# Three cross attentions opened inside the drains of the stages in front of them, in a twelve-stage decoder on one core

## The reference, cut to what matters

```python
x = _layernorm(x + _L0_attn_ref(x, ...))              # differential attention
x = _layernorm(x + _L0_xattn_ref(x, ctx_768, ...))    # scores clipped at 10000
x = _layernorm(x + _L0_ffn_ref(x, ...))               # two of eight experts
x = _layernorm(x + _L1_attn_ref(x, ...))              # rotary attention
x = _layernorm(x + _L1_xattn_ref(x, ctx_768, mask_BxS2_bf1, ...))
x = _layernorm(x + _L1_ffn_ref(x, ...))
x = _layernorm(x + _L2_attn_ref(x, ...))              # causal linear attention
x = _layernorm(x + _L2_xattn_ref(x, ctx_768, ctx_768, ...))
...

def _L2_xattn_ref(query, key, value, ...):
    Qp = query @ Wq + bq
    K = _l2norm(key @ Wk + bk)
    V = value @ Wv + bv
    Q = _l2norm(Qp)
    scores = jnp.einsum('bhqd,bhkd->bhqk', Q, K) * SCALE
    attn = jax.nn.softmax(scores, axis=-1)
    out = jnp.einsum('bhqk,bhkd->bhqd', attn, V)
    out = out @ Wo + bo
    x = out + Qp
    return (x - mu) / jnp.sqrt(var + LN_EPS) * ln_gamma + ln_beta
```

## Time and profile before

| what | value |
|---|---|
| median of 3 runs | 1764.18 us |
| lowest and highest | 1756.68 and 1767.77 us |
| the profiled execution | 1762.84 us, of which the span is 1761.1 us |
| TensorE (PE) busy in the span | 1565.7 us, 89% |
| VectorE (DVE), ScalarE (ACT), GpSimd (POOL) | 908.0, 679.4 and 412.6 us |
| mean granted TensorE clock | 0.959 of full speed |
| chain of waits, share by engine | PE 70%, DVE 11%, issue 8%, DMA 4% |

### The profile page before, as it was taken

How to read it: one execution, slowest core, us unless ns; L and a number is a source line. 1 busy time by engine, 2 the same in 40 slices (tenths; PEclk the granted TensorE clock), 3 DMA queues, 4 the chain that set the end, 5 groups by cost and what they waited for, 6 DMA issues and landing times.

```text
span 1761.1 us, 40069 instructions
## 1 busy us (share of the span) xinstructions
PE 1565.7 (89%) x14932; PEld 1292.9 (73%) x14932; DVE 908.0 (52%) x2316; ACT 679.4 (39%) x1611; POOL 412.6 (23%) x627
## 2 busy tenths in 40 slices
PE   7998998789995879998699598897998999999998
PEld 6876777678994757776589476775786776789897
DVE  3665787521105557777311363457444555565764
ACT  3334776322333327654123222553563443311110
POOL 2223776510005431111100243442121111000101
PEclk9998999999997999999899798999999999999999
DMA  5443000178971011110587201111001010033232
GB/s 204 148 153 135 28 27 16 49 291 293 319 250 46 1 42 41 30 29 12 229 293 275 75 1 33 41 40 49 1 1 62 28 42 1 25 111 105 88 104 69
DMA packets 41852, 166.76 MB, mean 95 GB/s; under 512 B 5984, under 2 KB 16864, under 8 KB 30176
## 3 DMA queue, kind: packets, MB, share of 16 engines
q1 hardware_dynamic: 39392, 159.14, 25.8%
q0 software_dynamic: 2304, 5.51, 1.0%
HBM read 140.22 MB, written 24.41 MB: 93 GB/s over the span
## 4 chain that ended last, share of the span: by engine, by line
PE 70%; DVE 11%; issue 8%; DMA 4%; POOL 3%; ACT 3%; SPq 1%; DVEq 0%; POOLq 0%; ACTq 0%
PE bank L1968 7%; PE bank L1981 7%; PE bank L1382 4%; PE bank L1910 4%; PE bank L1912 4%; PE bank L1911 4%; PE bank L1369 3%; PE bank L866 2%; PE bank L857 2%; PE bank L831 2%; PE bank L958 2%; PE bank L1352 2%; PE bank L1396 1%; PE bank L1357 1%; PE bank L1612 1%
## 5 line engine op out<-in xcount | busy, mean ns | idle before, releaser
L3597 POOL TENSOR_TENSOR mv<-mv,cst 112x1 f32<-112x1 f32 x88 | 22.5, 255 | 584.2 <-DVE mv L2631 584.2
L2336 ACT ACTIVATE arena<-big,nm 112x375 f32<-112x375 f32 x256 | 143.9, 605 | 25.9 <-DVE nm L3282 15.9
L2550 ACT ACTIVATE htile<-bank,wup 128x128 f32<-128x128 f32 x280 | 79.7, 368 | 189.6 <-PE bank L1968 189.6
L1968 PE MATMUL bank<-xtile,wup 128*128 128x128 f32 x1120 | 132.9, 278 | 0.3 <-DVE xtile L3444 0.2
L1382 PEld LDWEIGHTS bank<-cst,arena 112*125 112x125 f32 x768 | 100.1, 196 | 44.5 <-issue 21.9
L1968 PEld LDWEIGHTS bank<-xtile,wup 128*128 128x128 f32 x1120 | 129.9, 194 | 1.0 <-DVE xtile L3444 0.9
L3460 DVE COPY yrow<-bank 128x256 f32<-128x256 f32 x35 | 14.9, 425 | 217.6 <-PE bank L1981 217.6
L1981 PE MATMUL bank<-wdn,htile 128*128 128x256 f32 x560 | 126.3, 379 | 0.0
L1382 PE MATMUL bank<-cst,arena 112*125 112x112 f32 x768 | 115.3, 289 | 8.3 <-POOL arena L3763 4.7
L1981 PEld LDWEIGHTS bank<-wdn,htile 128*128 128x128 f32 x560 | 103.9, 190 | 12.8
L3763 POOL TENSOR_SCALAR arena<-arena,c_lo 112x375 f32<-112x375 f32 x64 | 98.0, 1544 | 37.1 <-ACT c_lo L2340 36.9
(11 more groups left out here) (386 smaller groups left out, 3735.8 us busy)
## 6 DMA issues: line engine op xcount, KB each, us to landing
wup<-in_moe_up SPq DMA_DIRECT2D x35, 1028.0 KB, 7.5
wdn<-in_moe_dn SPq DMA_DIRECT2D x35, 1024.0 KB, 5.5
vspace<-in_ring SPq DMA_DIRECT2D x40, 512.0 KB, 3.9
ctxs<-parts SPq DMA_DIRECT2D x30, 564.0 KB, 3.8
slots<-mlpw SPq DMA_DIRECT2D x11, 1024.0 KB, 6.3
parts<-ctxs SPq DMA_DIRECT2D x8, 564.0 KB, 3.1
xrow<-slots SPq DMA_DIRECT2D x35, 128.0 KB, 5.0
slots<-yrow SPq DMA_DIRECT2D x35, 128.0 KB, 7.1
```

What stands on the lines that cost most here:

```text
L1968: mm = pe.matmul(bank[2 + 2 * (g % 2) + m // 4][:, m % 4 * ROWS:(m % 4 + 1) * ROWS], wup[:, g % 3, k * HID + 128 * m:k * HID + 128 * m + 1 ...
L2336: nc.scalar.activation(c_pr[:, g, j, :], c_sc[:, g % 2, j, :], ACT.Exp, bias=nm[:, p, h:h + 1], scale=-1.0).then_inc(cexp_done, 1)
L2550: ins = nc.scalar.activation(htile[:, g % 2, m, :], bank[2 + 2 * (g % 2) + m // 4][:, m % 4 * ROWS:(m % 4 + 1) * ROWS], func, bias=wup[:, ...
```

## The change

It takes the code that opens stages 1, 4 and 7 out of these stages and puts it, cut into named pieces, into the drains of stages 0, 3 and 6, on TensorE, ScalarE, VectorE and GpSimd. The pieces replace filler matmuls. Some PSUM banks of the drains are changed to make room. The `split_kv` of stages 3 and 6 moves from the end of the stage to the end of step 1. In stage 7 ScalarE does its four exponentials in a run, and TensorE makes the first half of the next keys behind the values instead of in front of them. The core of the diff:

```diff
@@ TensorE, diff, step @@
-                            for _ in range(4):
-                                warm(bank[4], 512)
+                            cross(SUBS[sub.index + 1], "keys")
+                            cross(SUBS[sub.index + 1], "more keys")
                             pe.wait_ge(ln_dve, START + 3 * ln_unit(sub, b - 2) + 1)
                         output_columns_d(b - 1)
+                        if not back[0]:
+                            cross(SUBS[sub.index + 1], "queries")
@@ TensorE, causal, drain @@
                     if one:
-                        output_rows(sub, b - 1, bank[2])
-                        fillers(3)
-                        output_columns(sub, b - 1, bank[2])
+                        output_rows(sub, b - 1, OT)
+                        cross_normed(SUBS[sub.index + 1], "first")
+                        output_columns(sub, b - 1, OT)
+                        cross_normed(SUBS[sub.index + 1], "second")
+                        rows_t(sub, b - 2, p, bank[5])
+                        project_rows(sub, b - 1, OT)
+                        fillers(4)
                     else:
-                        fillers(3)
-                    rows_t(sub, b - 2, p, bank[5])
-                    if one:
-                        fillers(1)
-                        project_rows(sub, b - 1, bank[2])
+                        cross_normed(SUBS[sub.index + 1], "third")
+                        rows_t(sub, b - 2, p, bank[5])
+                        cross_normed(SUBS[sub.index + 1], "fourth")
@@ TensorE, rope, drain @@
                         values_turned(sub, b - 1, 1 - p)
+                        pe.wait_ge(xt_done, xt_at(sub, b - 3))
+                        cross(SUBS[sub.index + 1], "keys")
...
+                        output_rows(sub, b - 1, OT)
+                        cross(SUBS[sub.index + 1], "more keys")
+                        output_columns(sub, b - 1, OT)
+                        cross(SUBS[sub.index + 1], "queries")
+                        project_rows(sub, b - 1, OT)
+                        fillers(2)
@@ TensorE, cross_normed, pieces @@
+                if piece == "first":
+                    wait_weights(pe, sub)
+                    query_rows(0, 0)
+                    pe.wait_ge(part_low, B + 1 + sub.index // 3)
+                    keys(0, 0, 0, bank[0])
+                    return
+                if piece == "second":
+                    keys(0, 0, 1, bank[1])
+                    return
+                if piece == "third":
+                    pe.wait_ge(ln_dve, START + 3 * ln_unit(before, B - 2) + 1)
+                    queries_t(0, 0, TL)
+                    return
+                if piece == "fourth":
+                    key_sums(0, bank[4])
+                    return
@@ TensorE, cross_normed, step t = 0 @@
                             query_rows(b + 1, 1 - p)
-                            pe.wait_ge(cv_done, at(sub, "c3", b, 0))
-                            pe.wait_ge(cq_done, at(sub, "c1", 0, 1))
-                            keys(b + 1, 1 - p, 0, bank[5])
...
+                        if more:
+                            if one:
+                                pe.wait_ge(cv_done, at(sub, "c3", b, 0))
+                            else:
+                                wait_rows(pe, sub, B - 1)
+                            keys(b + 1, 1 - p, 0, bank[5])
@@ ScalarE and VectorE, rope and causal, step @@
-                    if isinstance(b, int) and b == B - 1:
+                    if isinstance(b, int) and b == 1:
                         split_kv(SUBS[sub.index + 1])
@@ VectorE, causal, drain @@
                     if one:
-                        output_normed(sub, b - 1, bank[2])
+                        output_normed(sub, b - 1, OT)
                     else:
-                        split_kv(SUBS[sub.index + 1])
+                        cross_normed(SUBS[sub.index + 1], "third")
                     rows_out(sub, b - 2, p)
@@ ScalarE, cross_normed, step @@
-                        exps(b, t, p, (0, 1))
-                    if t in (0, 1) and more:
+                        exps(b, t, p, (0, 1, 2, 3))
+                    if t == 1 and more:
                         keys(b + 1, 1 - p, t, bank[5])
...
+                    if back[0] and t < 2:
+                        value_rows(b, p, t, (TL, bank[4])[t])
+                    if t == 0 and more:
+                        keys(b + 1, 1 - p, t, bank[5])
@@ GpSimd, diff and rope, step @@
+                    if one and not back[0]:
+                        cross(SUBS[sub.index + 1], "queries")
```

181 lines of the change are left out of this document (115 added, 66 removed).

## The result

| | before | changed |
|---|---|---|
| median of the runs beside each other | 1765.97 us (4 runs, 1756.68 to 1767.99) | 1745.18 us (4 runs, 1735.58 to 1745.63) |
| ratio | | 0.9883, 95% interval 0.9844 to 0.9922 |
| profiled execution, span, clock | 1762.84, 1761.1, 0.959 | 1745.63, 1743.8, 0.956 |

The change makes the kernel 20.8 us faster, 1.2%. The forecast was 1743.0, out of terms that sum to -21. In a second comparison the changed kernel had 1739.8 us (6 runs) against 1763.4 (11 runs), ratio 0.987 (0.9841 to 0.9898).

What follows compares the result with a forecast made beforehand. TensorE was taken to be simply busy for most of the program, except in passages between stages. Terms -3.5, -6.55, +2.8, -8.7 and -5.0 gave -20.95, say -21 us, forecast 1743.0 us, range 1731 to 1755.

Steps and rivals of the forecast that it cites:

- Stage 0 to 1: Passage into stage 1: 4.5 us taken away, queries in front of the last projection cost 1.04; sum -3.5 us.
- Stage 3 to 4: Passage into stage 4: 5.95 us go, the split leaving the drain gives -0.9, longer queries cost +0.3; sum -6.55 us.
- The split in stage 3: Moved to step 1: VectorE waits for ScalarE's cast, delaying row 2's maxima; +2.8 us, bounds 0 and +4.5.
- rival A: Fewer fillers let TensorE's clock fall to half after pauses, taking some gain back: -11 us or 1753; chance 0.27.
- Stage 6 to 7: Passage into stage 7: 8.4 us removed, last rows_t 0.7 later, full clock -1.0; together -8.7 us, bounds -5.5 and -11.
- two-input rule: Stage 6's drain: normed queries on VectorE and GpSimd's root might exclude each other over SBUF; queries priced 0.35 to 1.6 us.
- Stage 7's loop: Context waits -6.1 and exponential waits 1.3 go, second keys' copy 1.2 later; -5.0 us, bounds -7.4 and +2.
- Elsewhere: Stages outside the edited ones: no term in the sum, since later weights and contexts are asked for by events that move along.
- signs of being wrong: Starts move but not the end, half clock in more stretches, or TensorE waits on stage 7's copy of keys.
- B: Stage 3's split finds VectorE free and half clock after the passage into stage 1 stays away: -26.3 us or 1737; chance 0.15.
- C: Stage 7's loop: later key copies chain up to 6.2 us per row over seven rows: +27 us or 1791; chance 0.05.
- D: Gains are waited for again at a load or in routing behind stages 1 and 4: about -8 us or 1756; chance 0.05.

Runs made afterwards that it cites:

- run 7: Changed kernel with the next stage's queries behind the last projection in stage 3's drain, TensorE's order alone: 1735.50 us, beside 1768.64 for the kernel before.
- run 8: Kernel before with fillers alone added between stages 6 and 7 (12 instead of 3, and 9 more): 1756.93 us, beside 1768.64 for the kernel before.
- run 2: Changed kernel with both edits of stage 7's loop undone and the three openings kept: 1741.55 us, beside 1759.24 for the kernel before.
- run 1: Changed kernel with ScalarE's cast for stage 3's split at the end of step 0 instead of step 1: 1737.31 us, beside 1759.24 before.
- run 3: Changed kernel with stage 7's next keys in front of the values again, exponentials kept in a run: 1747.18 us, beside 1759.24 before.
- run 9: Changed kernel with 6 fillers instead of 3 in rows 0 and 1 of stage 8: 1739.32 us, beside 1768.64 for the kernel before.

## Why the prediction was right, point by point

- **Stage 0 to 1: -3.5.** Measured -4.44 for the passage (-4.5), +0.87 from row 4 of the stage to its last (+1.04): -3.57 in this pair of profiles, -3.4 as the mean over the eleven. The price of the queries in front of the projection was right in size there. What I did not see is that it buys something: behind the projection they would hold GpSimd's root (run 7, shown in stage 3 only).
- **Stage 3 to 4: -6.55.** Measured -5.97 for the passage, against -5.95. A part of this is clock: in the run with fillers alone the passage of the kernel before took 52.54 us instead of 53.95, 1.4 less, without an edit in it. The drain gained 1.05 (7.99 us from its last row but one to the last in the kernel before, 6.94 in every run with the changed order), against my 0.6; in the changed kernel's own profile half clock at 641 took it back (+0.39 from row 0 to the last row).
- **The split in stage 3: +2.8.** The wait was right to 0.1 us (+2.86): the maxima of row 2 at 580.40, which is 584.4 less what was won before. But the term came out as +4.55, at my upper bound. This is the step of the sum whose mechanism failed. I had put the half clock, 1.7 us, into the bound and into rival A as a chance, and it belongs to the wait: every profile with this wait has half clock behind it (the segment 4.0 to 4.6 us longer in nine of nine). I read the price of a wait and not the price of what the wait does to TensorE's clock.
- **Stage 6 to 7: -8.7.** Measured -8.73 between last turned rows and first scores, but that is not the same sum. From start to start I had -8.4. Then +0.7 for late turned rows, which were not late at all: they come 4.05 us earlier than before (at 1071.17) where most of stage 6 was 3.75 earlier, so -0.3. And -1.0 for the clock, most of it on the first scores themselves, which is -0.83 (1.87 to 1.04 us) and lies behind their start. Like for like that is about -9.9, so the match of 8.7 and 8.73 is luck. Of the passage, 1.73 is clock by run 8. The normed queries, for which the prediction feared its two-input rule, took 0.35 us behind the statistics and not 1.59. They are also no case of the rule as it was put there: the instruction reads one tensor (L2993, `big<-big`). In the changed kernel it is the squares of the query row that take 0.92 us instead of 0.43 beside GpSimd.
- **Stage 7's loop: -5.0.** Measured -7.70 behind the first scores (0.83 of it the scores' own clock), and 7.45 by the loop's edits against run 2, at my lower bound of -7.4. This is the larger miss in size. The mechanism for the keys was right, and the size was off for two reasons. Row 0 waits longer for its context the earlier it starts (4.9 us, run 2), which a reading of the kernel before cannot show as a row. And I gave 1.3 us of gain to the run of exponentials, which costs 1.6. I had named its price, the late copy of the second keys, at 1.2 us, "and some of it will show"; it shows through another engine, as a collision of GpSimd with VectorE. So the two sizes were wrong in opposite ways: the keys are worth more than the 6.1 us of waits (9.1 with the exponentials interleaved), and the run of four less than nothing.
- **Elsewhere: 0.** Measured +0.8 from stage 4 to 6 and +3.7 in stage 8, both at half clock and both absent in other profiles of the same code. They took the profile pair to -17.3 where the medians have -20.8 and -23.6.

The errors were +1.75 for the split and -2.7 for the loop, and they nearly cancelled. That the medians stand where the forecast had them is in this part luck. Of the rivals, A was right about the step it named (the pause in stage 3), wrong for the passages into 4 and 7, where the clock rose. For stage 0 the pause that it feared came (2.84 us in front of the columns at 144.68, from 1.13), and in seven of eleven profiles of this code the drain then had a lower clock, though not in the changed kernel's own. Three of its signs of being wrong showed in part. Rows of stage 7 follow each other in 15.02 us and not in under 15. TensorE waits there for squares that start on the late copy of the keys (0.3 us each). And half clock came to stretches that had none (583.3 and 641.3), while it left the passages into 4 and 7; the mean over the span is 0.956 against 0.959. B's first half, the split for free, did not come true in this change and did in run 1. C decides from 2.3 us a row; the loop lost nothing. D is out: no wait for a load took a passage's gain back, and the 3.7 us lost in stage 8 are clock.

The affine took 917 ns beside GpSimd's squares and 425 without. The Trainium skill's page "SBUF — State Buffer", section "SBUF: two separate sides", has the rule for it that the prediction cited for the root: a VectorE instruction with two SBUF inputs and a GpSimd instruction that reads SBUF exclude each other. The trace agrees again. It was at hand for the loop too, had I followed the late copy to GpSimd.

## What to carry to other kernels

What does not need the last row of a stage can stand in the drain of that stage, and the passage then pays almost all that it took: here 4.4, 6.0 and 8.7 us, where the rows gave 4.5, 5.95 and 8.4, some 1.4 to 1.7 us of the last two being the clock that no longer falls there. A cross-engine pair such as cast and subtraction is to be placed by its first half: the second engine stands idle from its own place until the first one gets there, and everything in its queue with it. And a copy moved on an engine with time to spare should be followed through to who starts on it, since it can put two other engines on each other.

## What the runs showed of the hardware

- TensorE at half clock is part of a wait's price. In the changed kernel a pause of 1.99 us and VectorE's late maxima were followed by 6.8 us at 0.50. All nine profiles that had the wait had half clock behind it (0.89 to 0.95 granted over the segment of 32 us), and none of the four without it (1.00).
- The same kernel's two profiled executions lie 13.6 us apart in span, while segments with the same granted clock in both agree within 0.15 us. The shifts are 0.8 to 1.7 us each (in stage 8 1.70, 1.69 and 1.64 from row to row between these two). A difference of one profile pair in which the granted clock differs is not evidence, inside the edited segments (run 3 to row 0) or outside (run 9).
- GpSimd's squares beside VectorE's product of two SBUF tensors: 0.92 against 0.42 us for VectorE, 1.05 against 0.81 for GpSimd.
